# Layer 3's self-attention starts with the first batch element while layer 2's feed-forward outputs of the second are still made

## The reference, cut to what matters

```python
# layer 2, end
h = _ln(x, ln3_g, ln3_b)
x = x + (gelu(h @ fc1_w + fc1_b) @ fc2_w + fc2_b)
# layer 3, self-attention, 16 heads of 8 features, 512 keys
h1 = _ln(x, ln1_g, ln1_b)
q, k, v = h1 @ wq, h1 @ wk, h1 @ wv          # split in heads
sim = einsum(fq(q, dq), fq(k, dk)) * SCALE   # fq: round to 8-bit integers
attn = softmax(sim)
x = einsum(fq(attn, dw), fq(v, dv)) @ wo + bo + x
```

## Time and profile before

| what | value |
|---|---|
| median of 3 runs | 516.66 us (516.0 to 517.32) |
| the profiled execution | 517.13 us |
| its span in the trace | 515.2 us |
| busy: PE, DVE, ACT, POOL | 417.2, 354.7, 254.5, 238.2 us |
| first pair's maxima begin | 304.25 us |
| longest chain lines | L576 POOL 13%, L2168 DVE 9%, L885 PE 5% |

### The profile page before, as it was taken

How to read it: one execution, slowest core, us unless ns; L and a number is a source line. 1 busy time by engine, 2 the same in 40 slices (tenths; PEclk the granted TensorE clock), 3 DMA queues, 4 the chain that set the end, 5 groups by cost and what they waited for, 6 DMA issues and landing times.

```text
span 515.2 us, 8445 instructions
## 1 busy us (share of the span) xinstructions
PE 417.2 (81%) x2920; PEld 207.4 (40%) x2920; DVE 354.7 (69%) x804; ACT 254.5 (49%) x513; POOL 238.2 (46%) x376
## 2 busy tenths in 40 slices
PE   5999878898879999988898853666685677977897
PEld 2647545543434334343336530222232222433536
DVE  1755765769997114266864389999989997689552
ACT  2224444223003766624363338899987873457441
POOL 5042234365001445416011227999998886246420
PEclk9899999999999999999999895555555555689999
DMA  9500000000000000000000004797986867113401
GB/s 257 180 1 2 3 2 0 1 0 2 1 1 1 0 2 1 1 1 1 0 2 1 1 1 52 153 152 152 148 144 126 121 122 144 27 29 73 77 0 42
DMA packets 88975, 26.10 MB, mean 51 GB/s; under 512 B 81061, under 2 KB 88167, under 8 KB 88935
## 3 DMA queue, kind: packets, MB, share of 16 engines
q1 hardware_dynamic: 88935, 25.58, 25.8%
HBM read 5.61 MB, written 0.52 MB: 12 GB/s over the span
## 4 chain that ended last, share of the span: by engine, by line
PE 41%; DVE 28%; POOL 20%; issue 5%; ACT 2%; DMA 2%; POOLq 0%; DVEq 0%; ACTq 0%
POOL k_stack L576 13%; DVE k_stack L2168 9%; PE ps L885 5%; PE ps L900 4%; POOL stats L567 4%; PE ps L653 3%; PE ps L760 3%; DVE stats L2257 3%; PE ps L770 2%; PE ps L650 2%; DVE xh L1731 2%; PE ps L963 2%; PE ps L861 2%; DVE st L1722 2%; PE ps L633 2%
## 5 line engine op out<-in xcount | busy, mean ns | idle before, releaser
L2257 DVE TENSOR_REDUCE stats<-ps 128x2 f32<-128x1024 f32 x64 | 77.7, 1214 | 3.1 <-PE ps L1384 2.7
L1687 ACT ACTIVATE e_buf<-ps,stats,sders 128x512 f32<-128x512 f32 x88 | 67.6, 773 | 15.8 <-POOL stats L567 15.5
L576 POOL TENSOR_SCALAR k_stack<-e_buf,stats 128x512 int16<-128x512 f32 x88 | 62.8, 725 | 2.1 <-DVE stats L2264 1.5
L1402 PE MATMUL ps<-k_stack,q_stack 128*32 128x128 bf16 x512 | 38.3, 307 | 30.8 <-DVE k_stack L2270 30.6
L1533 ACT ACTIVATE e_buf<-ps 128x1024 f32<-128x1024 f32 (+3 forms) x44 | 28.2, 711 | 54.7 <-PE ps L885 54.7
L2168 DVE TENSOR_REDUCE k_stack<-ps 128x4 f32<-128x1024 f32 (+3 forms) x32 | 45.6, 1485 | 3.2 <-PE ps L827 3.2
L1384 PE MATMUL ps<-q_stack 32*128 32x512 bf16 x128 | 37.6, 588 | 12.4 <-ACT e_buf L1687 8.9
L433 POOL TENSOR_SCALAR_AFFINE_SELECT e_buf<-e_buf 128x256 f32<-128x256 f32 x44 | 17.7, 410 | 63.5 <-ACT e_buf L1533 62.8
L1402 PEld LDWEIGHTS ps<-k_stack,q_stack 128*32 128x32 bf16 x512 | 21.9, 129 | 62.0 <-DVE k_stack L2270 59.0
L484 POOL TENSOR_SCALAR rstd<-mv 128x4 f32<-128x4 f32 x18 | 4.4, 242 | 89.5 <-DVE mv L1725 89.5
L885 PE MATMUL ps<-k_stack,q_stack 32*128 32x512 f32 (+3 forms) x256 | 34.7, 478 | 0.6 <-ACT e_buf L1533 0.4
(11 more groups left out here) (288 smaller groups left out, 899.0 us busy)
## 6 DMA issues: line engine op xcount, KB each, us to landing
wsq<-in_squares SPq DMA_DIRECT2D x3, 384.0 KB, 5.0
k_stack<-k_stack SPq DMA_TRANSPOSE x64, 3.1
spread<-in_spread SPq DMA_DIRECT2D x1, 896.0 KB, 6.7
x<-in_x SPq DMA_DIRECT2D x1, 512.0 KB, 4.5
l_w<-in_L_xattn_W_ff SPq DMA_DIRECT2D x2, 256.0 KB, 7.1
l_w<-in_L_xattn_fc_w SPq DMA_DIRECT2D x2, 256.0 KB, 7.6
l_w<-in_L_xattn_ff_w SPq DMA_DIRECT2D x1, 512.0 KB, 8.6
out<-x SPq DMA_DIRECT2D x2, 256.0 KB, 2.3
```

The source lines that it names most:

```text
L576: pool.tensor_scalar(t_rows[n % TURNING][:, j, :], e_ring[n % len(e_ring)][:, j, :], stats[:, 2, c:c + 1], 0.0, ALU.mult, ALU.add).then_in ...
L1402: mm = pe.matmul(ps[BAND * band:BAND * (band + 1), 7 - b, qb * P:(qb + 1) * P], v_band[:, kb, b, V * band + v, :], t_keys[n % len(t_keys)] ...
L1687: act.activation(e_ring[n % len(e_ring)][:, j, :], ps[:, 2 * (n % 3) + j, :], ACT.Exp, bias=stats[:, 1, c:c + 1], scale=sders[:, 8:9], acc ...
L2257: dve.tensor_reduce(stats[:, 0, c:c + 2], ps[:, 2 * (n % 3):2 * (n % 3) + 2, :], AX, ALU.max, negate=True).then_inc(S("ints.nm"), 1)
```

## The change

The first half's entry to layer 3 (transposes into bank 6, queries, keys, values into banks 2, 4 and 7) goes ahead of the second half's output products on TensorE. Of those, tiles 0 and 1 are made before the first scores and tiles 2 and 3 in step 2, in bank 6. All that follows for the second half goes into steps of the pairs: DVE's addition in step 2, moments in step 3, norm in step 5; POOL's deviation in step 4, bias in step 9; TensorE's transposes in step 9; ACT's copy after the exponentials of step 10; query, key and value projections in steps 13, 18 and 23 between scores and outputs, all in bank 6; their reads by DVE in steps 14, 19 and 24, the integers one step later; the key masks move to steps 6, 11, 17 and 26 to 29. The ring of exponentials begins with its two places in `t_buf`, and pair 2 waits until the last output product has been made.

```diff
+LATE_ADDED, LATE_MOMENTS, LATE_NORMAL, LATE_READ = 2, 3, 5, (14, 19, 24)
+LATE_RSTD, LATE_BIAS, LATE_TURNED, LATE_STATE, LATE_PROJECTED, LATE_BANK = 4, 9, 9, 10, (13, 18, 23), 6
...
+        int_ring = e_ring[4:] + e_ring[:4]
...
 # POOL: shift_pairs, step n, behind shift(n) and rounded(n - 3)
+                    if n == LATE_RSTD:
+                        rstds_of("L3.ln1", 1)
+                    if n == LATE_BIAS:
+                        add_bias("L3.ca0", "L3.ln1.xh", 1, B)
...
 # PE
-                out_rows("L2.ff", l2_w2, 1, OUTPUTS_2)
-                for k in range(B):
-                    turn_half(xh, "L3.ln1.xh", k)
-                    qkv("L3.sa", W["L3_xattn_a1_wq"], W["L3_xattn_a1_wk"], W["L3_xattn_a1_wv"], k)
+                turn_half(xh, "L3.ln1.xh", 0, bank=LATE_BANK)
+                pe.wait_ge(S("state.T"), state("L3.sa", 0))
+                pe.wait_ge(S("ff.hid"), count("L2.ff", "hid") + B * FC)
+                project("L3.sa", W["L3_xattn_a1_wq"], 0, 2).then_inc(S("L3.sa.q.mm"), 1)
+                project("L3.sa", W["L3_xattn_a1_wk"], 0, 4).then_inc(S("L3.sa.k.mm"), 1)
+                int_values(0, 7)
+                out_rows("L2.ff", l2_w2, 1, LATE_BANK - 1, range(2))
...
                     if n < PAIRS:
                         int_scores(n)
+                    if n == 2:
+                        out_rows("L2.ff", l2_w2, 1, LATE_BANK - 1, range(2, QB))
+                    if n == LATE_TURNED:
+                        turn_half(xh, "L3.ln1.xh", 1, bank=LATE_BANK)
+                    if n == LATE_PROJECTED[0]:
+                        pe.wait_ge(S("state.T"), state("L3.sa", 1))
+                        project("L3.sa", W["L3_xattn_a1_wq"], 1, LATE_BANK).then_inc(S("L3.sa.q.mm"), 1)
+                    if n == LATE_PROJECTED[1]:
+                        pe.wait_ge(S("L3.read"), 1)
+                        project("L3.sa", W["L3_xattn_a1_wk"], 1, LATE_BANK).then_inc(S("L3.sa.k.mm"), 1)
+                    if n == LATE_PROJECTED[2]:
+                        pe.wait_ge(S("L3.read"), 2)
+                        int_values(1, LATE_BANK)
...
 # ACT
-                state_out("L3.sa", col("L3_xattn_ln1_g"), col("L3_xattn_ln1_b"))
+                state_out("L3.sa", col("L3_xattn_ln1_g"), col("L3_xattn_ln1_b"), [0], LATE_BANK)
                 for n in range(PAIRS):
                     act.wait_ge(S("ints.m"), n + 1)
+                    if n == 2:
+                        act.wait_ge(S("add.o"), count("L2.ff", "o") + B)
...
+                    if n == LATE_STATE:
+                        state_out("L3.sa", col("L3_xattn_ln1_g"), col("L3_xattn_ln1_b"), [1], LATE_BANK)
...
 # DVE: prepare(n), behind maxima(n)
+                    if n == LATE_ADDED:
+                        add_to_x("L2.ff", LATE_BANK - 1, [1])
+                    if n == LATE_MOMENTS:
+                        moments("L3.ln1", 1, "L2.ff.x", 1)
+                    if n == LATE_NORMAL:
+                        normal("L3.ln1", 1)
+                    if n in LATE_READ[:2]:
+                        read_late(LATE_READ.index(n))
+                    if n == LATE_READ[0] + 1:
+                        dve.wait_ge(S("L3.read"), 1)
                         integers(half(q_int, 1), half(ta, 1))
+                    if n == LATE_READ[1] + 1:
+                        dve.wait_ge(S("L3.read"), 2)
                         integers(half(k_int, 1), half(tb, 1))
+                    if n == LATE_READ[2]:
+                        read_values(1)
+                    if n == LATE_READ[2] + 1:
+                        values(1)
+                    if n in (6, 11, 17):
+                        key_mask((6, 11, 17).index(n) + 1)
+                    if LATE_READ[2] + 2 <= n < LATE_READ[2] + 2 + V:
+                        key_mask(V + n - LATE_READ[2] - 2)
...
 # DVE, before the first pair: the queries and keys of the first half alone
-                read_queries_and_keys(1)
```

More of the change, by code:

```diff
@@ L575, in rounded @@
                         c = 2 * (n % 8) + j
-                        pool.tensor_scalar(t_rows[n % TURNING][:, j, :], e_ring[n % len(e_ring)][:, j, :],
+                        pool.tensor_scalar(t_rows[n % TURNING][:, j, :], int_ring[n % len(int_ring)][:, j, :],
                                           stats[:, 2, c:c + 1], 0.0, ALU.mult, ALU.add).then_inc(S("ints.rounded"), 1)
@@ L613, in _ @@
             if stop >= 3:
-                for h in range(B):
-                    rstds_of("L3.ln1", h)
-                    add_bias("L3.ca0", "L3.ln1.xh", h, h + 1)
+                rstds_of("L3.ln1", 0)
+                add_bias("L3.ca0", "L3.ln1.xh", 0, 1)
                 shift_pairs()
@@ L753, in single_head, with out_rows @@
                 outputs(2 * T - 1)
-            def out_rows(name, w2, k, bank=4):
+            def out_rows(name, w2, k, bank=4, tiles=range(QB)):
                 pe.wait_ge(S("ff.hid"), count(name, "hid") + FC * (k + 1))
-                for t in range(QB):
+                for t in tiles:
                     o = ps[:, bank + k, t * P:(t + 1) * P]
@@ L760, in out_rows @@
                         mm = pe.matmul(o, tile(hid[:, c, :], k * QB + t), w2[:, c, :], start=(c == 0), stop=(c == FC - 1))
-                mm.then_inc(S("add.o"), 1)
+                if t == QB - 1:
+                    mm.then_inc(S("add.o"), 1)
             def hidden_blocks(name, w1, banks, blocks):
@@ L788, in gated_feed_forward, with int_values @@
                     out_rows(name, w2, k)
+            def int_values(k, bank):
+                for t in range(QB):
+                    o = ps[:, bank, t * P:(t + 1) * P]
+                    mm = pe.matmul(o, tile(xT, k * QB + t), W["L3_xattn_a1_wv"], start=True, stop=True)
+                mm.then_inc(S("L3.sa.v.mm"), 1)
             def project_half(name, wo, k, bank):
@@ L1377, in int_scores @@
                     pe.wait_ge(S("L3.kmask"), b * V + v + 1)
-                    if n < 3:
-                        pe.wait_ge(S("L3.read"), n)
                     if n >= 3:
@@ L1391, in int_outputs @@
                     pe.wait_ge(S("L3.values"), b + 1)
-                    if n == 0:
-                        pe.wait_ge(S("L3.v.read"), B)
+                    if n % (PAIRS // B) == 0:
+                        pe.wait_ge(S("L3.v.read"), b + 1)
                     if n % (PAIRS // B) == 0:
@@ L1678, in _ @@
             if stop >= 3:
-                state_out("L3.sa", col("L3_xattn_ln1_g"), col("L3_xattn_ln1_b"))
+                state_out("L3.sa", col("L3_xattn_ln1_g"), col("L3_xattn_ln1_b"), [0], LATE_BANK)
                 for n in range(PAIRS):
                     act.wait_ge(S("ints.m"), n + 1)
-                    if n >= len(e_ring):
-                        act.wait_ge(S("ints.rounded"), 2 * (n - len(e_ring) + 1))
+                    if n == 2:
+                        act.wait_ge(S("add.o"), count("L2.ff", "o") + B)
+                    if n >= len(int_ring):
+                        act.wait_ge(S("ints.rounded"), 2 * (n - len(int_ring) + 1))
                     for j in range(2):
                         c = 2 * (n % 8) + j
-                        act.activation(e_ring[n % len(e_ring)][:, j, :], ps[:, 2 * (n % 3) + j, :], ACT.Exp,
+                        act.activation(int_ring[n % len(int_ring)][:, j, :], ps[:, 2 * (n % 3) + j, :], ACT.Exp,
                                        bias=stats[:, 1, c:c + 1], scale=sders[:, 8:9],
                                        accum_out=stats[:, 3, c:c + 1]).then_inc(S("ints.exp"), 1)
+                    if n == LATE_STATE:
+                        state_out("L3.sa", col("L3_xattn_ln1_g"), col("L3_xattn_ln1_b"), [1], LATE_BANK)
                     if n == PAIRS // B + VALUES_BEHIND - 2:
@@ L2182, in _ @@
                 cross_heads()
[L2183 to L2187, removed]
+                add_to_x("L2.ff", OUTPUTS_2, [0])
+                if stop >= 3:
+                    moments("L3.ln1", 0, "L2.ff.x", 1)
+                    normal("L3.ln1", 0)
             if stop >= 3:
@@ L2195, in bounded, with read_queries_and_keys, read_late @@
                     then(dve.tensor_scalar(tmp, tmp, MAGIC - ZERO_POINT, MAGIC + QMAX - ZERO_POINT, ALU.max, ALU.min))
[L2197 to L2206, removed]
-                    else:
-                        then(ins)
+                def read_queries_and_keys():
+                    dve.wait_ge(S("L3.sa.q.mm"), 1)
+                    scaled(half(ta, 0), ps[:, 2, :], DQ1)
+                    dve.wait_ge(S("L3.sa.k.mm"), 1)
+                    then(scaled(half(tb, 0), ps[:, 4, :], DK1))
+                def read_late(part):
+                    if part == 0:
+                        dve.wait_ge(S("L3.sa.q.mm"), B)
+                        scaled(half(ta, 1), ps[:, LATE_BANK, :], DQ1).then_inc(S("L3.read"), 1)
+                    else:
+                        dve.wait_ge(S("L3.sa.k.mm"), B)
+                        scaled(half(tb, 1), ps[:, LATE_BANK, :], DK1).then_inc(S("L3.read"), 1)
```

(17 more changed lines are left out.)

## The result

The changed kernel takes 519.67 us (median of 13 runs), the kernel before 517.32 (13 runs of the same session). The ratio is 1.0041 (95% interval 1.0023 to 1.006), 1.2 to 3.1 us: slower by 2.35 us, where 1.3 was forecast, and inside the range (513.2 to 521.0).

A forecast was written before the change was run, and what follows sets the result against it. DVE was taken to set the pace in the first 13 pairs, with DVE and POOL both full in the next 17. Entry -7.05, DVE's work +1.9 and waits +6.45 gave +1.3: 518.0 us median, range 513.2 to 521.0.

The forecast's parts named there:

- Entry: Stretch ahead of the pair loop: first maxima at 297.2 instead of 304.25, a gain of 7.05 us.
- Norm in step 5: In step 5 DVE, there at 308.0, waits 2.3 us for POOL's deviation, done at 310.2.
- Step 13 (wait 2): At pair 13, POOL's chain with the bias delays the maxima to 324.0; DVE, done by 323.0, waits 1.0 us.
- Projections: Steps 13, 18, 23: projections of about 2.0 us between scores and outputs cause waits of 1.35, 0.75, 1.05, together 3.15.
- VectorE's work: First maxima to pair 30's: 4.4 us moved in makes DVE's work 58.2 against 56.32 before, +1.9 us.
- rival C: Work between pairs pays loop prices if POOL is in a rounding: together +3.0, 521.0; chance 0.18.
- Rival A: In the pairs POOL sets the pace, so only its additions of 2.62 count: -4.4, 512.3; chance 0.18.
- Rival B: The three late projections fit TensorE's idle time, other terms stand: -1.85, 514.8; chance 0.14.

The follow-up runs named there:

- light VectorE run: Changed kernel with VectorE's added addition, norm and late reads cut to two columns, moments to one tile: stretch to pair 30 62.72 us, ratio to before 0.9991.
- light projections: Changed kernel with the second half's three late projections multiplying 32 columns each instead of 512: stretch to pair 30 63.44 us, ratio to before 0.9989.

## Why the prediction came out as it did

The direction and the outline were right: an early start of 7 us, given back between the pairs with some more. The closeness of the sum is in part luck: VectorE's work was put 3.1 us too low and the waits 1.7 too high. Term by term, to pair 30:

- **Entry.** -7.05 forecast, -7.23 measured.
- **Norm in step 5.** Wait of 2.3 forecast, 2.17 measured, at the forecast place and with the forecast releaser. What its removal is worth was less (1.44), for the reason above.
- **Step 13 (wait 2).** 1.0 forecast; there was none. The maxima of pair 13 started right behind VectorE's work. VectorE was itself late: it had lost 0.93 in step 10 beside the bias, 0.16 before the maxima of pair 9, and 0.24 before those of pair 10, whose scores came behind the transposes that I had costed at nothing. The stretch to pair 13 came out at 27.87, 1.1 above my 26.8, and by another way, so that its being near is luck.
- **Projections.** Waits of 1.35, 0.75 and 1.05 forecast; 0.79, 0.59 and 0.79 measured. The length I took, 2.0, was right (2.01); the phase was not. Cut to 32 columns they give back 2.56, against 3.15.
- **VectorE's work.** This is the mis-sized term. Forecast 58.2 us for the stretch without new waits; measured 66.00 less the waits of 2.17, 0.79, 0.59, 0.79, 0.16 and 0.24, which is 61.3. The work that moved in was sized rightly: addition 0.68, moments 1.24, norm 1.11 and two reads 1.48 make 4.5, against 4.4. What came out dearer was what had been there. The 24 bounds of turned weights took 11.9 us against 10.2 before (1.35 beside the bias; 0.75 and 0.80 in steps 14 and 24), the 14 products of the reciprocals 3.0 where my 0.15 for each makes 2.1, and the seven key masks 3.4 against 3.1. I had given all of them the price that they have beside an idle GpSimd, and rejected the dearer one in rival C because GpSimd would be idle after the wait. It was, for the norm; it was not in the steps that followed.

Sum: 64.7 forecast for the stretch, 66.0 measured; +1.3 forecast, +2.4 measured. Rival A (GpSimd's pace) is refuted by the light VectorE run and by GpSimd's gaps. Rival B (projections hide) is refuted by the light projections, though in twelve parts they do almost hide. Rival C was right in its mechanism, though the instructions that paid were for the most part others than it named, and it was too high in its sum (521.0).

## What to carry to other kernels

An early start pays only what the pipeline behind it can carry: add up the work that moves into the loop on the engine that sets its pace, and take it at the price it has beside the other engines, not alone. Work fitted into an engine that does not set the pace was paid here where it came in one piece of 2.0 us, with waits of 0.6 to 0.8 for each, and nearly vanished in quarters of 0.73. When such work is split or moved, look again at what feeds it: with one copy put a step later, waits of 0.3 to 0.9 stood behind the first parts and looked like their price. Where a clock dip elsewhere moves a span by more than the change, compare starts of the same instruction inside the stretch, not spans.

## What the runs showed that I had not expected

The fall of the clock in the hidden blocks comes and goes with the same instructions: 5.40 in eight of the eleven profiles, 3.70 in the first profile of the changed kernel, in that with the norm in step 7 and in the last. TensorE was idle for 0.87 us just ahead of the blocks with and without the dip. The cause of the difference stays open. It did not touch the comparison of the stretches. Nor did a second difference: in the changed kernel's first profile the clock was 0.85 from 338 to 342 us and 0.50 in the second, with 66.00 and 65.89 for the stretch; the three late projections took 2.0 in both. In the pairs the clock fell to its lower level at about 300 in the changed kernel and at about 309.5 before, some 5 us after the first maxima in both.
